# Attention and feed-forward kernel on one core: two kinds of waits moved inside their steps

## The reference, cut to what matters

```python
h = shift_token(x)                  # second half of the features comes from the token before
q, k, v = split(h @ wqkv)           # 8 heads of 64
q, k = rotary(l2norm(q)), rotary(l2norm(k))
x = x + local_attention(q, k, v) @ wo           # windows of 64, the one before included
h = shift_token(x)
h = (h - mean(h)) / sqrt(var(h) + 1e-5) * lg + lb
a, g = split(h @ w1 + b1)
x = x + (a * gelu(g)) @ w2 + b2
```

## Time and profile before

| | |
|---|---|
| three runs | 1524.20, 1524.51 (median), 1526.63 us |
| the profiled execution | 1523.33 us |
| its span, first to last instruction | 1521.5 us |
| mean granted clock of PE | 0.972 |
| busy: DVE, PE, ACT, POOL | 1385.0 (91%), 1345.4 (88%), 1334.6 (88%), 1198.6 us (79%) |
| chain that ended last, by engine | DVE 53%, PE 14%, ACT 13%, issue 10%, DMA 7%, POOL 2% |

### The profile page before, as it was taken

The page is one execution under the profiler, slowest core; times in us unless marked ns, Lnnn a source line. Parts: engine busy times, 40 slices in busy tenths (PEclk is TensorE's granted clock), DMA queues, the critical chain, the costliest instruction groups (busy, mean ns, idle before and its releaser), DMA issues.

```text
span 1521.5 us, 40000 instructions
## 1 busy us (share of the span) xinstructions
PE 1345.4 (88%) x14680; PEld 1095.8 (72%) x14680; DVE 1385.0 (91%) x2245; ACT 1334.6 (88%) x4080; POOL 1198.6 (79%) x1383
## 2 busy tenths in 40 slices
PE   1666989999999999999999999999999998789995
PEld 1455767787777877778777877778777877667774
DVE  3999999999999999999999999999999997678851
ACT  1365989999999999999999999999999999599993
POOL 2857988888898888888988888888988886488740
PEclk9597999999999999999999999999999999999998
DMA  5021112131122213122122213122121213011220
GB/s 165 10 39 33 29 38 37 48 62 43 24 57 45 55 30 61 40 43 57 24 58 45 44 40 62 41 36 49 37 58 37 51 34 61 11 30 24 44 51 29
DMA packets 177636, 67.81 MB, mean 45 GB/s; under 512 B 146934, under 2 KB 152355, under 8 KB 177443
## 3 DMA queue, kind: packets, MB, share of 16 engines
q1 hardware_dynamic: 176146, 64.70, 20.1%
q10 hardware_dynamic: 1296, 0.56, 0.1%
HBM read 17.54 MB, written 8.39 MB: 17 GB/s over the span
## 4 chain that ended last, share of the span: by engine, by line
DVE 53%; PE 14%; ACT 13%; issue 10%; DMA 7%; POOL 2%; SPq 1%; DVEq 0%; POOLq 0%; ACTq 0%
DVE sb_t L818 7%; DMA sb_x<-sb_x 7%; DVE sb_qk L813 6%; DVE sb_nml L833 6%; DVE sb_pr L789 6%; DVE banks L794 5%; ACT sb_pl L647 4%; DVE sb_ssq L828 4%; DVE banks L778 3%; DVE sb_hid L867 2%; PE banks L1004 2%; ACT sb_gate L683 2%; PE banks L994 2%; PE banks L894 2%; ACT sb_hn L670 2%
## 5 line engine op out<-in xcount | busy, mean ns | idle before, releaser
L647 ACT ACTIVATE sb_pl<-banks,sb_nml 128x128 f32<-128x128 f32 x1024 | 362.6, 398 | 9.4 <-DVE sb_nml L833 8.9
L561 POOL TENSOR_TENSOR sb_qk<-sb_qk,sb_t 128x1024 f32<-128x1024 f32 x128 | 304.1, 2381 | 13.4 <-DVE sb_t L818 13.4
L556 POOL TENSOR_TENSOR sb_pr<-sb_qkvf 128x2048 f32<-128x2048 f32 x64 | 293.1, 4579 | 3.8 <-DVE banks L778 3.8
L647 ACT ACTIVATION_READ_ACCUMULATOR sb_pl<-banks,sb_nml 128x1 f32 x1024 | 244.8, 239 | 0.0
L574 POOL TENSOR_TENSOR sb_qk<-sb_qk,sb_rn 128x1024 f32<-128x1024 f32 x128 | 242.4, 1905 | 1.4
L654 ACT ACTIVATE sb_pl<-sb_pl,sb_rl 128x128 f32<-128x128 f32 x640 | 211.8, 451 | 2.6 <-DVE sb_rl L838 2.6
L894 PE MATMUL banks<-sb_wqh,sb_hh 128*128 128x512 f32 x384 | 173.4, 452 | 28.3 <-DVE sb_t L818 25.4
L624 ACT ACTIVATE sb_sq<-banks 128x1024 f32<-128x1024 f32 x128 | 134.6, 1052 | 40.5 <-PE banks L896 39.0
L833 DVE TENSOR_REDUCE sb_nml<-banks 128x4 f32<-128x512 f32 x256 | 163.9, 683 | 6.0 <-PE banks L972 5.9
L600 ACT ACTIVATE sb_pT<-banks 128x512 f32<-128x512 f32 x256 | 155.5, 653 | 11.9 <-PE banks L983 11.6
L818 DVE TENSOR_TENSOR sb_t<-banks,sb_tab 128x512 f32<-128x512 f32 x256 | 163.9, 683 | 0.0
(11 more groups left out here) (118 smaller groups left out, 3519.3 us busy)
## 6 DMA issues: line engine op xcount, KB each, us to landing
sb_vs<-sb_v SPq DMA_DIRECT2D x224, 128.0 KB, 2.4
sb_xt<-x SPq DMA_DIRECT2D x16, 256.0 KB, 3.4
heads_scratch<-sb_ofs SPq DMA_DIRECT2D x64, 64.0 KB, 3.6
sb_orow<-heads_scratch SPq DMA_DIRECT2D x16, 256.0 KB, 3.4
sb_ob<-x SPq DMA_DIRECT2D x16, 256.0 KB, 2.9
out<-sb_ob SPq DMA_DIRECT2D x16, 256.0 KB, 2.4
sb_hh<-sb_sh SPq DMA_DIRECT2D x16, 128.0 KB, 2.4
sb_hl<-sb_sl SPq DMA_DIRECT2D x16, 128.0 KB, 2.4
```

The costliest lines, as they stand in the source:

```text
L556: nc.gpsimd.tensor_tensor(pr[:].rearrange("p (q k d) -> p q k d", q=H, k=H), q[:, :, None, :].to_broadcast([P, H, H, D]), k[:, None, :, :] ...
L561: nc.gpsimd.tensor_tensor(qk[:, k, :], qk[:, k, :], t2[:, TURN[step] % 2, :], ALU.add).then_inc(s_add.sem, 1)
L647: last = nc.scalar.activation(pl[:, k, m, :], ps[:, m * P:(m + 1) * P], ACT.Exp, bias=nml[:, k, m:m + 1], accum_out=suml[:, k, m:m + 1])
```

## The change

`stats2` first waits for `x2` (DVE's own earlier step), issues the `bn_stats` of blocks 1 to 3, then waits for the DMA and issues that of block 0. `qkv_full`, `project_qk` of layer 1, and the first part of `up` wait at their head for the high part alone; the wait for the low part goes between the second and the third product. In `up` the order of the products changes too, so that the one with the low part is last. Nothing is added or taken away but waits.

```diff
                 if kind == "stats2":
...
+                    rows = x2[:, TURN["x2", s, l, 0] % 2, :, :]
+                    dve.wait_ge(s_x2.sem, s_x2.at(same("x2", step, 0), step))
+                    for b in range(1, NB):
+                        nc.vector.bn_stats(st2[:, b, :], shifted(rows, b))
                     dve.wait_ge(s_hs.sem, s_hs.at(same("shift_x2", step, 0), step))
-                    for b in range(NB):
-                        last = nc.vector.bn_stats(st2[:, b, :], shifted(x2[:, TURN["x2", s, l, 0] % 2, :, :], b))
+                    last = nc.vector.bn_stats(st2[:, 0, :], shifted(rows, 0))
                     last.then_inc(s_bn2.sem, 1)
...
-            def parts3(dst, ah, al, bh, bl):
+            def parts3(dst, ah, al, bh, bl, low=None):
+
                 mm(dst, ah, bh, start=True, stop=False)
                 mm(dst, ah, bl, start=False, stop=False)
+                if low:
+                    pe.wait_ge(*low)
                 return mm(dst, al, bh, start=False, stop=True)
...
                 if kind == "qkv_full":
                     claim(step)
-                    pe.wait_ge(s_xlow.sem, s_xlow.at(("x_low", s, 0, 0), step))
+                    pe.wait_ge(s_xhigh.sem, s_xhigh.at(("x_split", s, 0, 0), step))
...
+                    low = (s_xlow.sem, s_xlow.at(("x_low", s, 0, 0), step))
+                    parts3(ps[:, 0:3 * E], sh[:, o], sl[:, o], w3h[:], w3l[:], low).then_inc(s_qkvf.sem, 1)
                 if kind == "project_qk":
...
-                        pe.wait_ge(s_x1l.sem, s_x1l.at(("x1_low", s, 0, 0), step))
+                        pe.wait_ge(s_x1h.sem, s_x1h.at(("x1_split", s, 0, 0), step))
...
+                        low = (s_x1l.sem, s_x1l.at(("x1_low", s, 0, 0), step)) if l and not k else None
+                        last = parts3(qk_ps[:, o], hh[:, u, c], hl[:, u, c], wqh[:, l, o], wql[:, l, o], low)
...
                 if kind == "up":
                     if n == 0:
                         in_order(in_unit_before("down", step, 0), step)
-                        pe.wait_ge(s_l2.sem, s_l2.at(same("low2", step, 0), step))
+                        pe.wait_ge(s_h2.sem, s_h2.at(same("high2", step, 0), step))
...
                     for k in range(2):
                         claim(step, k)
-                        parts3(bank(step, k), wuh[:, l, 1 - k, o], wul[:, l, 1 - k, o], mh[:], ml[:]).then_inc(s_up.sem, 1)
+                        ps, a = bank(step, k), 1 - k
+                        mm(ps, wuh[:, l, a, o], mh[:], start=True, stop=False)
+                        mm(ps, wul[:, l, a, o], mh[:], start=False, stop=False)
+                        if n == 0 and k == 0:
+                            pe.wait_ge(s_l2.sem, s_l2.at(same("low2", step, 0), step))
+                        mm(ps, wuh[:, l, a, o], ml[:], start=False, stop=True).then_inc(s_up.sem, 1)
```

More of the change, by code:

```diff
@@ L926, in _ @@
                     o = slice(n * P, (n + 1) * P)
-                    parts3(ps[:, 0:3 * E], sh[:, o], sl[:, o], w3h[:], w3l[:]).then_inc(s_qkvf.sem, 1)
+                    low = (s_xlow.sem, s_xlow.at(("x_low", s, 0, 0), step))
+                    parts3(ps[:, 0:3 * E], sh[:, o], sl[:, o], w3h[:], w3l[:], low).then_inc(s_qkvf.sem, 1)
                 if kind == "project_qk":
@@ L941, in _ @@
                         o = slice(k * INNER, (k + 1) * INNER)
-                        last = parts3(qk_ps[:, o], hh[:, u, c], hl[:, u, c], wqh[:, l, o], wql[:, l, o])
+                        low = (s_x1l.sem, s_x1l.at(("x1_low", s, 0, 0), step)) if l and not k else None
+                        last = parts3(qk_ps[:, o], hh[:, u, c], hl[:, u, c], wqh[:, l, o], wql[:, l, o], low)
                     last.then_inc(s_qk.sem, 1)
```

## The result

The changed kernel takes 1512.05 us (median of 6 runs, 1510.07 to 1513.98); the kernel before, beside it on the same chip, 1524.65 (6 runs, 1523.6 to 1526.63). The ratio is 0.9915, with a 95% interval of 0.9902 to 0.9928. The forecast was 1513.7, in a range of 1507.0 to 1520.5. The profiled execution has 1510.4 us and a span of 1508.6, 12.9 under the 1521.5 of before. The six runs of the changed kernel lie in two groups, three from 1510.07 to 1510.80 with a mean granted clock of 0.974 or 0.975 and three from 1513.31 to 1513.98 with 0.968 or 0.969; the profile shows one of the first group, and no profile shows where the 3 us of the second lie.

What follows compares the result with a forecast made beforehand. DVE was taken as full except where the change works, with ACT limiting what it can gain. Regular layer-0 units 5.9, irregular units 1.2 and last units 3.7 sum to 10.8 us: 1524.5 - 10.8 = 1513.7, range 1507.0 to 1520.5.

Steps and rivals of the forecast that it cites:

- The cover, 0.59 us: In `stats2`, three `bn_stats` starting 0.197 apart cover 0.59 us of DVE's wait for the DMA of shifted rows.
- Layer 0 counts, layer 1 does not: In the regular stretch, `stats2` gains 0.59 us per layer-0 unit, 5.9 for ten, and nothing in layer 1.
- DVE would only come 0.38 us too early: In layer 1, DVE reaches the third `hid` 0.38 us sooner but must wait there for `gelu`; gain nothing.
- ACT's reserve in layer 0, 0.67 us: ACT's steps around `norm2` up to the third `gelu` can come 0.09 + 0.38 + 0.20 = 0.67 us earlier.
- Irregular units, 1.2 us: Six `stats2` waits before or just after the regular stretch: half the cover for four of them, 1.2 us.
- `up` in the regular stretch, nothing: The first bank of `up` is full 0.46 us earlier, but `gelu` comes later anyway, so nothing is gained.
- `qkv_full`, `project_qk`, nothing: Two products move ahead of the low part in `qkv_full`; neither there nor in `project_qk` is anything gained.
- The last units, 3.7 us: Late serial units gain from statistics and `up`: 0.8 + 1.05 + 0.6 + 1.28 = 3.7 us.
- Added waits, nothing: Waits between products in `qkv_full`, `project_qk` and `up` cost PE between 0 and 0.11 us each; taken as 0.
- everything counting: Rival: layer 1's third `gelu` also comes earlier, so small waits count throughout the kernel; 1507.7 us, chance 0.16.
- ACT taking it all: Rival: ACT or another loop lets layer 0 gain nothing, leaving only the end's 3.7 us; 1520.8 us, chance 0.14.
- the strict form: On DVE, each `bn_stats` starts only on an empty pipeline: four last 1.11 us, cover 0.83; judged not to hold.

Runs made afterwards that it cites:

- the scaling moved off ACT: The changed kernel with the fourth scaling of the probabilities on GpSimd instead of ScalarE: 1509.12 us, ratio 0.9883.
- the aggregations ahead: The changed kernel with the aggregation of blocks 1 to 3 also put before the wait for the shifted rows: 1512.63 us, ratio 0.9908.
- ACT relieved: The changed kernel with the fourth scaling on GpSimd and the aggregation of blocks 1 to 3 before the wait for shifted rows: 1507.24 us, ratio 0.9891.
- the products alone: The changed kernel with the statistics put back, all four blocks behind the wait for the shifted rows: 1524.16 us, ratio 0.9981.
- a cure tried alone: The kernel before with only the fourth scaling of the probabilities moved from ScalarE to GpSimd: 1525.68 us, ratio 1.0012.

## Why the prediction was right, point by point

**The cover, 0.59 us.** Right: three statistics took 0.58 off the wait in layer 0, and one took 0.20 off. The step fell by 0.57.

**Layer 0 counts, layer 1 does not.** Right, and shown by the two kernels that have it in one layer: steps 85.72 and 86.29. The cause given for layer 1, ACT's run up to the third `gelu`, is shown by the scaling moved off ACT, under which layer 1 gains too. "DVE would only come 0.38 us too early" came out as two waits, 0.15 and 0.33.

**ACT's reserve in layer 0, 0.67 us.** It held the 0.57. That it is nearly used up is borne out by the aggregations ahead: at most 0.1 with ACT as it is, 0.21 in layer 0 with ACT relieved. Of the 0.67, the last 0.20 rested on overlaps that the earlier trace rows shows only in part; the layer-0 half of the pair fell by 44.16 - 43.49 = 0.67 us with the aggregations ahead and no further, which bears out the sum.

**Irregular units, 1.2 us: too small.** The step that failed is "I take half of the cover for four of them". Five units gave 2.5 together, four of them nearly the full cover or all of it (0.53, 0.54, 0.58, 0.59).

**`up` in the regular stretch, nothing.** Right: 86.25 with the products alone.

**`qkv_full`, `project_qk`, nothing.** Right within what the runs can tell. The first `qkv_full` began 0.3 us earlier (28.09 against 28.39, now behind the split of the weights), and the next wait, for `hl`, grew from 2.93 to 3.44.

**The last units, 3.7 us: came to 4.8**, with errors both ways. Units at 1312, 1382, 1424, 1464: forecast 1.05, 0.3, 0, 0.3, measured 0.76, 0.31, 0.00, 0.33. Unit at 1276: 0.8 against 1.62; last one: 1.28 against 1.8. Each term was made of delays taken off a serial chain, and two things failed. For the unit at 1276 it was "less what ACT holds back: 0.8". The products alone gave their whole 0.46 there, and with the 0.59 of the statistics that is 1.05; the three kernels with both edits whose clock fell in that unit, as it did in the kernel before, gave 1.04, 1.12 and 1.35. The other thing is the granted clock, which stands in the sum only for the two products of the last unit. The changed kernel's profile kept its clock full in the unit at 1276, which fits the remaining 0.3 to 0.6 us. In the last unit three products fewer ran at the low level, 0.6 us, which with 0.53 from DVE (`x2` to `aggr2` took 1499.55 - 1494.40 = 5.15 us before, 1487.91 - 1483.29 = 4.62 after) and 0.7 from the first product makes the 1.8. The two forecast parts of that unit, 0.59 and 0.69, were right; the 0.6 is the clock's. What decides where the clock falls stays open: it is not the pause before `up` alone, as the waits of 0.74 and 1.53 above show.

**Added waits, nothing.** Right, and for waits already met bounded by 0.006 us, far below 0.11.

**Sum.** 10.8 forecast, 12.9 in the two profiles, 12.6 between the medians. Two terms were too small, 1.2 against 2.6 and 3.7 against 4.8, which is 2.5 us; the regular units and the start each lacked 0.2. The profile is of the group of runs at 1510 us, so part of the late units' share may be the luck of one execution; the group at 1513.3 to 1514.0 lies around the forecast. The other rivals: with everything counting a pair would have taken 85.3, with ACT taking it all 86.2; it took 85.67.

**The two statements cited.** By the Trainium skill ("VectorE: DVE Perf Modes", "The DRAIN you can't avoid") a DVE instruction starts only on an empty pipeline, unless nothing holds it; the strict form would have given a cover of 0.83. The wait fell by 0.58, and three statistics again last 0.67 and not 3 x 0.28, so the trace decides against the strict form here. By the Trainium skill ("TensorE: Matmul & The Clock Gate", "Architectural detail: the array is 16× 32×32, not 1× 128×128") PE's queue can pull weight loads ahead of products in flight. The trace agrees: the load at 598.97 lies beside the second product, ahead of a wait inside the group.

## What to carry to other kernels

Where a full engine waits for a transfer that only part of its next step needs, put the rest of the step ahead of the wait, and count the gain by the distance between starts, not by durations. Before that, read the engine that feeds back to it: the gain stops at that engine's reserve, which here was put at 0.67 us in one kind of unit and at none in the other, and the runs bore it out (0.57 to 0.67 gained, and 0). Where two limits lie side by side, a cure tried alone and found worthless (ratio 1.0012) can be worth 0.6 us a pair once the other is cured.

## What the runs showed that I had not expected

The clock as a term of the sum. In the serial stretches of these kernels the granted clock was low after PE's long pauses, and the first products after one stood 0.43 us apart instead of 0.23. How many did so in the last unit, whose 18 products of `up` are the same in all fourteen kernels, varied from 6 or 7 to 14, some 1.4 us between them, which is more than the edits bring at that place. With three blocks ahead, `up` as changed and no scaling moved it was 6 to 8, in six kernels; what sets it was not found.

A run of like DVE instructions is worth keeping together. With the aggregations split, in layer 1, where no wait was to be covered, statistics and aggregations took 1.20 us instead of 1.07, counted from start to start. Undone in that layer, the step fell from 84.94 to 84.84.

The start scatters: at the 6th unit the kernels stand between 1.2 us ahead of and 2.1 behind the kernel before, with no relation to their edits. Why was not tried.
